# A masked attention kernel: GpSimd codes in one pass, nodes loaded twice, the y product written to PSUM at a step of four

## The reference

```
h      = max(layernorm(x), 0)
scores = where(adj > 0, h @ weight @ input.T, -2**32 + 1)
atten  = softmax(scores / 0.07, axis=1)
out    = x + atten @ input
```

## Time and profile before

| | |
|---|---|
| median of three runs | 925.26 us (925.25 to 925.46) |
| span of the profiled execution | 922.5 us, 26099 instructions |
| PE busy | 906.1 us (98%) |
| DVE busy | 814.5 us (88%) |
| ACT busy | 744.0 us (81%) |
| POOL busy | 705.6 us (76%) |
| HBM read, written | 160.50 MB, 3.15 MB |

### The profile page before, as it was taken

The page is one execution under the profiler, slowest core; times in us unless marked ns, Lnnn a source line. Parts: engine busy times, 40 slices in busy tenths (PEclk is TensorE's granted clock), DMA queues, the critical chain, the costliest instruction groups (busy, mean ns, idle before and its releaser), DMA issues.

```text
span 922.5 us, 26099 instructions
## 1 busy us (share of the span) xinstructions
PE 906.1 (98%) x7566; PEld 659.9 (72%) x7566; DVE 814.5 (88%) x1626; ACT 744.0 (81%) x1468; POOL 705.6 (76%) x587
## 2 busy tenths in 40 slices
PE   7989999999999999999999999999999999999997
PEld 4466777777777777777777777777777777777776
DVE  6998889988998899889988998898889888988985
ACT  5987888888888888888888888888888888888885
POOL 5999878787778877887788778877887788788712
PEclk9999999999999999999999999999999999999999
DMA  9789999999999999999999999999999999999965
GB/s 343 232 224 257 279 267 278 257 287 266 286 278 267 272 273 273 267 272 273 276 273 267 269 274 274 275 260 276 276 268 265 276 274 278 260 270 269 278 105 100
DMA packets 360361, 242.46 MB, mean 263 GB/s; under 512 B 321808, under 2 KB 340368, under 8 KB 341904
## 3 DMA queue, kind: packets, MB, share of 16 engines
q1 hardware_dynamic: 353136, 238.87, 100.9%
q10 hardware_dynamic: 7200, 3.28, 1.5%
HBM read 160.50 MB, written 3.15 MB: 177 GB/s over the span
## 4 chain that ended last, share of the span: by engine, by line
PE 93%; DVE 2%; DMA 2%; SPq 2%; issue 1%; ACT 0%; DVEq 0%; ACTq 0%
PE ps_s L900 38%; PE ps_o L948 26%; PE ps_o L950 13%; PE ps_t L923 13%; DMA pT_dma<-split 2%; SPq L353 1%; PE ps_t L967 1%; DVE probs L695 1%; PE ps_s L977 1%; DMA nodes_raw<-in_L_gnn_input_dram 0%; DVE v L763 0%; DVE pT_lo L718 0%; DVE split L724 0%; PE ps_o L967 0%; DVE pT_hi L714 0%
## 5 line engine op out<-in xcount | busy, mean ns | idle before, releaser
L695 DVE CUSTOM_DVE_ANT_0 probs<-ps_s,absent 128x1024 f32<-128x1024 f32 x288 | 351.4, 1220 | 49.6 <-PE ps_s L900 42.8
L900 PE MATMUL ps_s<-yT_hi,hT 128*128 128x512 f16 x1152 | 389.2, 379 | 1.0 <-DVE chunk_max L695 0.9
L460 POOL TENSOR_SCALAR absent<-present 128x2048 bf16<-128x2048 bf16 x141 | 294.3, 2087 | 34.9 <-POOL present L451 34.3
L587 ACT ACTIVATE pT_hi<-ps_t 128x512 f16<-128x512 f32 x281 | 167.7, 597 | 156.0 <-PE ps_t L923 155.9
L451 POOL TENSOR_SCALAR present<-adj_i 128x2048 bf16<-128x2048 int32 x144 | 273.6, 1900 | 13.3 <-DMA adj_i<-in_adj_dram 13.3
L948 PE MATMUL ps_o<-v,pT_dma 128*128 128x256 f16 x1152 | 222.1, 273 | 5.2 <-DMA pT_dma<-split 2.9
L557 ACT ACTIVATE ps_t<-probs,neg_max,exp_scale 128x512 f32<-128x512 f32 x285 | 220.3, 773 | 2.6 <-DVE neg_max L705 1.2
L900 PE MATMUL ps_s<-yT_lo,hT 128*128 128x512 f16 x576 | 218.3, 379 | 0.0
L718 DVE TENSOR_TENSOR pT_lo<-ps_t,pT_hi 128x512 f16<-128x512 f32 x284 | 194.3, 684 | 21.8 <-ACT pT_hi L587 20.4
L948 PE MATMUL ps_o<-v,pT_hi 128*128 128x256 f16 x1152 | 205.9, 273 | 0.9 <-DVE pT_lo L718 0.8
L950 PE MATMUL ps_o<-v,pT_dma 128*128 128x128 f16 x1152 | 206.5, 220 | 0.0
(11 more groups left out here) (82 smaller groups left out, 508.8 us busy)
## 6 DMA issues: line engine op xcount, KB each, us to landing
adj_i<-in_adj_dram SPq DMA_DIRECT2D x144, 1024.0 KB, 5.3
pT_dma<-split SPq DMA_TRANSPOSE x288, 3.5
nodes_raw<-in_L_gnn_input_dram SPq DMA_DIRECT2D x6, 512.0 KB, 6.7
x_res<-in_x_dram SPq DMA_DIRECT2D x48, 64.0 KB, 3.9
out_dram<-fin ACTq DMA_DIRECT2D x48, 64.0 KB, 2.5
x_ln<-in_x_dram SPq DMA_DIRECT2D x46, 64.0 KB, 5.0
hT<-h_split SPq DMA_TRANSPOSE x45, 5.0
x_ln<-in_x_dram ACTq DMA_DIRECT2D x2, 64.0 KB, 3.0
```

The source lines that it names most:

```text
L460: nc.gpsimd.tensor_scalar(by_block(absent[:, c, :]), by_row(flags(s, c)), -ABSENT, ABSENT, ALU.mult, ALU.add).then_inc(absent_done, 1)
L587: nc.scalar.activation(pT_hi[:, p % BANKS, :], turn_area(k, at), ACT.Copy).then_inc(hi_done, 1)
L695: nc.vector.tensor_tensor_reduce(out=probs[:, s, j * SCORE:(j + 1) * SCORE], in0=ps_s[j % 2][:, :], in1=absent[:, c, part * SCORE:(part + ...
L900: made = nc.tensor.matmul(ps_s[j % 2][:, q * 512:(q + 1) * 512], hT[:, s, part, :], y[:, cols], start=(part == 0 and y is yT_hi), stop=(pa ...
```

## The change

- The two POOL passes become one, `convert` (a tensor_scalar, int32 in, uint32 out, contiguous on both sides): adj x -2^40 + 2^39, so 0 gives the largest uint32 and 1 gives 0. `absent` and `present` (bf16) go; `codes` (uint32, three chunks) comes. DVE's mask reads `codes`. The scales of h and y shrink to fit.
- ACT's `early_absent` (three instructions in the head) goes.
- Columns now stand in the order of the nodes: `make_y` reads a turn of `nodesT` block by block and writes PSUM at a step of four elements.
- v needs natural order too, so `nodes` are loaded a second time: six parts into the same `nodes_raw`, in runs of 512 bytes. SP issues part i when PE has turned it and DVE has its maximum. These six stand on SP's queue behind `x_res` of tile 0 and ahead of `x_ln` of tiles 2 and 3 and of `early_adj`. ACT's `v_hi` waits for the second load.
- All four parts of v's low half are made by POOL; DVE's `v_lo` goes. POOL's order in the head becomes: codes of tile 0 (three), v part 0, codes (1,0), v part 1, codes (1,1), codes (1,2), h of tile 2, codes (2,0), v part 2, codes (2,1), v part 3.
- `w`, `wT`, `spread_w` and `spread_nodes` share memory with the last DMA transpose buffer.

```diff
-    H_SCALE = 2.0 ** 12
-    Y_TOP = 14
+    H_SCALE = 2.0 ** -3
+    Y_TOP = 3
-    ABSENT = 2.0 ** 64
+    PRESENT_STEP = -2.0 ** 40
+    ABSENT = 2.0 ** 39
...
-    nodes_v = nodes.rearrange("(j g p b) d -> j p g (b d)", g=1024 // TURN, p=P, b=PER_TURN)
+    runs_v = nodes.rearrange("(j g p b) d -> j p g (b d)", g=1024 // TURN, p=P, b=PER_TURN)
+    nodes_v = nodes.rearrange("(j b p) d -> j p b d", p=P, b=NODE_PART)
...
             sp.dma_start(x_res[:, 0, :], x_v[0]).then_inc(x_res_in[0], 16)
+            for i in range(NODE_PARTS):
+                blocks = slice(i * NODE_PART, (i + 1) * NODE_PART)
+                sp.wait_ge(nodes_turned, (i + 1) * NODE_PART // PER_TURN)
+                sp.wait_ge(part_max_done, i + 1)
+                sp.dma_start(nodes_raw[:, blocks, :], nodes_v[i]).then_inc(nodes_in[i], 16)
             for u in range(2, 4):
                 sp.wait_ge(h_done, u - 1)
                 load_x(u, u % 2)
             def early_adj(n):
-                sp.wait_ge(present_done, n + 1)
+                sp.wait_ge(coded, n + 1)
                 load_adj(n // CONVS + 1, n % CONVS)
...
-            def find_present(u, s, c):
+            def convert(u, c):
                 pool.wait_ge(adj_in[c], u * 16 + 16)
...
+                if not (isinstance(u, int) and u == 0):
                     pool.wait_ge(masked, u * SCORES + (PER_CONV * (c + 1) - SCORES))
                 pool.sem_inc(pool_waited, 1)
-                nc.gpsimd.tensor_scalar(by_block(absent[:, c, :]), by_row(flags(s, c)), -ABSENT, ABSENT,
-                                        ALU.mult, ALU.add).then_inc(absent_done, 1)
+                nc.gpsimd.tensor_scalar(codes[:, c, :], adj_i[:, c, :], PRESENT_STEP, ABSENT, ALU.mult, ALU.add)\
+                    .then_inc(coded, 1)
...
+                for n in range(i * PART // NODE_PART, -(-(i + 1) * PART // NODE_PART)):
+                    act.wait_ge(nodes_in[n], 32)
                 nc.scalar.activation(v[:, blocks, 0, :], nodes_raw[:, blocks, :], ACT.Copy, scale=scale)\
                     .then_inc(v_hi_done, 1)
...
-                    in0=ps_s[j % 2][:, :], in1=absent[:, c, part * SCORE:(part + 1) * SCORE],
+                    in0=ps_s[j % 2][:, :], in1=codes[:, c, part * SCORE:(part + 1) * SCORE],
...
-                nc.tensor.matmul(y_bank[k % Y_BANKS][:, :], wT[:, :], nodesT[:, k * TURN:(k + 1) * TURN],
+                nc.tensor.matmul(by_key(y_bank[k % Y_BANKS][:, :]), wT[:, :],
+                                 by_block(nodesT[:, k * TURN:(k + 1) * TURN]),
                                  start=True, stop=True).then_inc(y_made, 1)
```

More of the change, by code:

```diff
@@ L21, in gnn_masked_attention_kernel @@
     fp32 = mybir.dt.float32
-    bf16 = mybir.dt.bfloat16
     fp16 = mybir.dt.float16
     int32 = mybir.dt.int32
+    uint32 = mybir.dt.uint32
     ALU = mybir.AluOpType
@@ L117, in gnn_masked_attention_kernel @@
         adj_i = sb("adj_i", [P, CONVS, CONV], int32)
-        absent = sb("absent", [P, CONVS, CONV], bf16)
-        present = sb("present", [P, 2, CONV], bf16)
+        codes = sb("codes", [P, CONVS, CONV], uint32)
         pT_hi = sb("pT_hi", [P, BANKS, TURN], fp16)
@@ L166, in gnn_masked_attention_kernel @@
         exp_scale = sb("exp_scale", [P, 1], fp32)
-        spread_w = sb("spread_w", [P, P], fp32)
-        spread_nodes = sb("spread_nodes", [P, P], fp32)
+        head_only = pT_dma[:, D_HALVES - 1, :, :].rearrange("p b n -> p (b n)").bitcast(fp32)
+        w, wT, spread_w, spread_nodes = [head_only[:, i * P:(i + 1) * P] for i in range(4)]
         nodesT = probs[:, 1, :]
@@ L291, in turn_area, with by_key @@
             return ps_t[k % BANKS][:, :]
+        def by_key(part):
+            return part.rearrange("q (p b) -> q b p", b=PER_TURN)
         def by_block(part):
-            return part.rearrange("q (g b p) -> q g b p", b=PER_TURN, p=P)
-        def by_row(part):
-            return part.rearrange("q (g p b) -> q g b p", b=PER_TURN, p=P)
+            return part.rearrange("q (b p) -> q b p", b=PER_TURN)
         def has(at, ahead):
@@ L495, in _ @@
             for c in range(CONVS):
[L496 to L504, removed]
+                convert(0, c)
             v_lo_pool(0)
-            pool.wait_ge(absent_done, 4)
-            find_present(1, 1, 2)
-            make_absent(1, 1, 2, True)
+            convert(1, 0)
+            v_lo_pool(1)
+            convert(1, 1)
+            convert(1, 2)
             make_h(2, 0)
-            find_present(2, 0, 0)
-            v_lo_pool(1)
-            find_present(2, 0, 1)
+            convert(2, 0)
             v_lo_pool(2)
+            convert(2, 1)
+            v_lo_pool(3)
             def step(t, par, at):
@@ L593, in y_hi @@
                                      scale=y_scale).then_inc(y_hi_done, 1)
-            def early_absent(u, c):
-                act.wait_ge(present_done, u * CONVS + c + 1)
-                act.wait_ge(masked, u * SCORES + (PER_CONV * (c + 1) - SCORES))
-                nc.scalar.activation(by_block(absent[:, c, :]), by_row(present[:, (u + c) % 2, :]), ACT.Identity,
-                                     bias=absent_top[:, :], scale=-ABSENT).then_inc(absent_early_done, 1)
             for u in range(2):
@@ L617, in _ @@
                     v_hi((k - 5) // 2)
-            act.wait_ge(top_set, 1)
-            early_absent(1, 1)
             for g in range(2):
@@ L633, in step @@
                 for z in range(CYCLES):
-                    if at == 0 and z > 0:
-                        early_absent(2, z - 1)
                     hi_p(t, CYCLE * z, at)
@@ L756, in y_lo @@
                     .then_inc(y_lo_done, 1)
-            def v_lo(k):
-                dve.wait_ge(v_hi_done, k // PART_TURNS + 1)
-                dve.wait_ge(scale_steps, 4)
-                blocks = slice(k * PER_TURN, (k + 1) * PER_TURN)
-                nc.vector.scalar_tensor_tensor(out=v[:, blocks, 1, :], in0=nodes_raw[:, blocks, :], scalar=scale,
-                                               in1=v[:, blocks, 0, :], op0=ALU.mult, op1=ALU.subtract)\
-                    .then_inc(v_lo_done, 1)
             def y_scales():
@@ L862, in step @@
                         invert_sum(t, par)
-                    if at == 0 and z == 1:
-                        v_lo(FIRST_V_VECTOR + 1)
                     lo_p(t, CYCLE * z, at)
-                    if at == 0 and z == 1:
-                        v_lo(FIRST_V_VECTOR + 2)
                     for q in range(2):
@@ L882, in step @@
                                 invert_sum(t, par)
-                            if at == 0 and z == 0:
-                                v_lo(FIRST_V_VECTOR)
             steps(dve, step)
```

58 lines of the change are left out of this document (10 added, 48 removed).

## The result

Over eleven runs of each on one chip the changed kernel takes 927.12 us (median; 925.48 to 930.01), the kernel before 925.25 us (924.26 to 926.68): ratio 1.0020, 95% interval 1.0011 to 1.0028. It is 1.9 us slower, inside the range and 0.6 us above the forecast. The interval excludes no change, if only by a little. The profiled execution took 927.55 us, with a span of 925.6: 3.1 us more span than before, where +1.2 was forecast.

The account below looks back on a forecast made before the run. PE bounds the kernel, busy 99 to 100 of 100 us from 60 to 860 us, so only the first 62 us count. +5.2 - 4.0 = +1.2 takes the span from 922.5 to 923.7, median 926.5; range 922.9 to 931.5.

Parts of the forecast that it names:

- Two terms of opposite sign: In the head: second load delays tile 0's maximum, +5.2 us; removed v_lo and early_absent give -4.0; sum +1.2.
- The load's first effect: In the head: 10.8 us of load hold x_ln to 31.2; DVE waits, tile 0's maximum moves +5.2 us.
- the clock would fall behind the first stall and cost nothing: PE idles from 29.5 to about 33, its clock may fall; DVE bounds the next masks, so costed at nothing.
- The step that failed: In the head: the load's cost taken as the maximum's delay through DVE's wait for x_ln, +5.2 us.
- The relief: At product 4: without DVE's v_lo and ACT's early_absent, 2.3 us of stall and 1.7 of clock go, 4.0 in sum.
- the y step: y product's PSUM write at a step of four: costed at nothing, bound from above +4.2 us.
- the mask: DVE's mask with four-byte codes: taken as unchanged at 1220 ns for 1024 elements.
- POOL: One 2.06 us pass replaces two, gain nothing; v part 3 done at 60.8, margin 1.5 us ahead of product 9.
- Rival 1: In the head: x_ln wait doesn't bite; ACT's v_hi(0) delays by 2.4 us instead; 922.8 us, chance 0.13.
- rival 2: y product's stepped PSUM write takes 1.72 us instead of 0.86: +4.2 over the sum, 930.7 us, chance 0.12.
- rivals 3 and 4: POOL's uint32 pass above 2.06 us: 929.7 or 934.7, chance 0.10; mask over a quarter slower: 960 or more, chance 0.02.
- The bridge from span to median: Whole run: the median lies 2.8 us above the profiled span, so a span of 923.7 becomes 926.5.

Follow-up runs that it names:

- run 8: Changed kernel without the second load of nodes and ACT's wait for it (attention sum is not the reference's): 921.54 us, ratio 0.9948 to the kernel before.
- run 2: Kernel before plus only the second load of nodes, with ACT's v_hi waiting for it (attention sum is not the reference's): 933.51 us, ratio 1.0075.
- run 1: Changed kernel with x_ln of tiles 2 and 3 issued ahead of the second load of nodes, nothing else: 928.45 us, ratio 1.0016 to the kernel before.
- run 6: Changed kernel with x_ln first, adj loads interleaved with the second load, POOL's codes (1,1) ahead of v part 1, v_hi pieces rearranged: 926.48 us, ratio 1.0005.
- run 5: Kernel of run 1 with POOL making codes (1,1) ahead of v part 1: 928.27 us, ratio 1.0026 to the kernel before.
- run 7: Kernel of run 6 with the load of adj (2,1) moved behind the first DMA transposes: 927.98 us, ratio 1.0024 to the kernel before.
- run 9: Changed kernel with the low half of v's part 1 made by DVE again, in three pieces at their old places: 930.08 us, ratio 1.0048.
- run 3: Changed kernel with the y product written contiguously, without the step of four (scores masked at other places): 928.55 us, ratio 1.0018.

## Why the prediction was right, and where its working was not

**The sign and the place were right.** Two terms of opposite sign, the load's above the relief's: by run 8 and run 2 the load costs 6.7 and 6.9 us, and the rest of the change gives 4.8 (run 8 against before) and 5.1 us (run 2 against after). The prediction had +5.2 and -4.0. It is short by some 1.6 us on the load and 1 on the relief, each known within 2 us; as these errors have opposite signs, the net of +1.9 stands near the +1.2. That is partly luck.

**The load's first effect was right in nearly every step:** 10.8 us long, its transfers ahead of x_ln's, DVE waiting to 30.8, the maximum at 40.88, the first transposes issued at 44.36 (forecast 44.3). The adj of tile 1 was there for POOL at 33.68 (forecast 34.0). Missed was where x_ln waits: ahead of its issue, at SP, for the most part, and not in the queue. That the clock would fall behind the first stall and cost nothing was right too.

**The step that failed** is that the load's whole cost was the maximum's delay, through the x_ln wait. By it run 1 would have gained (up to 2.9 us, by its maximum); it gained nothing measurable. The prediction followed x_ln and adj past the new loads, and didn't ask what 10.8 us more work do to the queue once the wait is gone. Runs 6 and 8 show it: with the maximum and SP's issue where they were before, product 0 still waits 3.44 us for the queue; without the load it waits 0.52. What doesn't fit comes out as transposes landing late, at product 0 or further on. In the changed kernel as it is, the maximum's delay, with the x_ln wait in it, covers nearly all of this cost, 5.75 of 6.3 us, which is why the sum came near.

**The clock is part of what the reordered kernels pay.** The stalls that runs 1, 5, 6 and 7 move to other places are followed by a fallen clock where PE, and not DVE, sets the pace. By the starts of the same matmuls in both traces this costs 2.6, 1.7, 1.4 and 1.7 us. By subtraction, an estimate, runs 1 and 6 would without it lie some 3 us below the changed kernel instead of 0.4 and 1.4. So it isn't the queue's length alone that makes these orders come out so nearly equal, and no run here holds the clock fixed to separate the two.

Which link holds the queue back in run 1 is only argued: there the DMA share falls to 0.55 from 38 to 44 us, so POOL's codes and SP's order hold it there rather than its own length. In the changed kernel it is 0.51 in the same stretch. In run 6 the share has no gap.

**The relief** was given as 2.3 of stall and 1.7 of clock. In the trace it is 3.33 and 1.69, so 5.0. Run 9 gives 2.6 for the v_lo alone, without a clock term, because no clock falls in that run: 2.6 plus the 1.7 of before's clock is 4.3. The 0.5 to 0.8 left of 4.8 to 5.1 is less than the intervals can tell from nothing, and was not isolated; `early_absent` is in it, which the prediction named and gave no price of its own.

**Costed at nothing, and rightly:** the y step (run 3); the mask (1220 to 1221 ns); POOL, whose pass took 1.90 and not 2.06 us, so that v's last part was done at 59.70 and product 9 at 62.87 left a margin of 3.2 us instead of 1.5. Rival 1 is excluded by the wait of 3.77 us for x_ln (the wait for ACT that it names is there as well, and is what run 1 is left with), rival 2 by run 3, rivals 3 and 4 by the 1901 and 1221 ns. "Granted clock 1.00 from 45 us on" held too.

**The bridge from span to median.** The profiled execution has 1.95 us around its span, not the 2.8 that came from setting one span of before against the median of other runs. By spans the forecast was 1.9 us too low, by medians 0.6. Executions of the kernel before in the later sets lie 1.7 to 1.9 us above their spans; by that its profiled one took about 924.3 us, 1 us under its median, and so much of the 3.1 us of span isn't the change's. The nearness by medians is in part chance.

## What to carry to other kernels

When a transfer is added, find the first wait that it makes, and then add up the queue: its length against the idle share up to the next transfer that somebody awaits. What doesn't fit is paid even when that first wait is moved away: of the four reorderings here, one gained 1.4 us and none the 6.7 that the load costs. Look at the granted clock behind each new place of the stall too. A layout that spares the transfer (here one load in shorter runs, 1.5 us later at the maximum instead of 5.2) was worth more than any order tried here.

## What the runs showed of the hardware beyond that

- A PSUM write at a step of four behaves as a limit of 0.43 us per 512 columns, and not as a surcharge: fp32 matmuls at 0.43 don't notice it, fp16 ones go from 0.22 to 0.43.
- 512-byte runs move at 290 GB/s, in the load as in the lone store of the earlier trace rows; the adj loads behind them at 418 (32 to 38 us of the changed kernel).
- POOL's int32 pass takes 1.90 us per 2048 elements with two bytes or four out.
- PE idle for 2.22 us is followed by a granted clock of 1.00 in run 9, idle for 2.26 us by 0.54 in the kernel before: a stall of the same length doesn't always cost the clock. PE was fully busy from 50 to 52 us and then idle 3.6 us of twelve in run 9; in the kernel before it was busy 5.6 of the 6 us ahead of 50, then idle. Run 9 also keeps 1.00 over 26 to 40 us, behind a first stall of 3.74 us, where the changed kernel, with 4.36, falls to 0.50.
